# Inverted row sums 16 wide, their spreading on ScalarE, and turned probabilities copied by one engine

## The chip, the cores and the metric

The kernel runs on one core of a Trainium2 chip. The metric is the device time of one execution in microseconds (us), as the median of several runs. Engines are named as in the profile: PE is TensorE's matmuls, PEld its weight loads, DVE is VectorE, ACT is ScalarE, POOL is GpSimd, SP is the engine whose queue starts the DMAs.

## The reference, cut to what matters

Four cross-attention layers act in a chain on x of 4 batches x 1024 tokens x 256, each with 77 keys made from a context of its own batch. The first has 8 heads of 32 and is followed by a state-space scan over the tokens; the second has 16 heads of 64 and a causal mask; the third and the fourth have 16 heads of 16, with a mask each, and the fourth ends in an MLP with a GELU. What the change is about is the softmax and what follows it:

```
# layer 3 of the chain (L2 in the code), 16 heads of 16
m = max(scores, -1)
e = exp(scores - m) * mask
probs = e / (sum(e, -1) + 1e-09)
attn = einsum('bhqk,bhkd->bhqd', probs, vh)      # then @ Wo.T + bo, + residual, layer norm
# layer 4 of the chain (L3 in the code), 16 heads of 16
attn = softmax(where(xa_mask, neg, attn), -1)
out = einsum('bhnm,bmhd->bnhd', attn, v)         # then @ proj_w + proj_b, + x, MLP
```

The kernel leaves the division until after the product with the values: it multiplies each head's 16 output columns by 1 / sum.

## The kernel before, in words

Tokens are worked on in tiles of 128. There are 32 tiles, spread over four lanes; a lane has two PSUM banks of its own (2 * lane and 2 * lane + 1) and its own slice of every SBUF buffer. The first phase (until about 250 us of the span) takes each tile through layer L0 and prepares the scan; the scan runs over all tokens; the second phase takes each tile through L1, L2, L3 and the MLP. Tables of keys and values for L1 to L3 are made for one pair of batches ahead of the second phase, and for the other pair in its middle.

The steps of a lane are a list (`attention_steps`, `lane_steps`), and so are the table building ("a", "b"), the set-up ("i") and the scan ("s"). `MADE_BY` gives each step to one engine. `TURNS` has one string for each engine, written out: character by character it says whose next step the engine issues. So every engine has one fixed order, and the steps wait for each other through semaphores, `done[step]`, that are compared with a step's number in its engine's order.

The steps around the change, for L2 and L3 (`a.name` is "2" or "3"), each for two groups of 8 heads (".0" and ".1"):

- `scores` (PE, L860) fills both banks with 8 x 77 scores; `bound` (DVE, L1378 and L1381) masks them into SBUF; `rowmax` (DVE, L1388), `below` (POOL, L1663), `expo` (ACT, L1196) give the exponentials; `maskmul` (POOL, L1649) is for L2 alone; `rowsum` (DVE, L1399) writes the 8 sums of the group into `mx`.
- `pturn` (PE, L875) turns the 616 probability columns in five tiles of 128, the last with 104 rows. Four go to the lane's first bank, the fifth to the second.
- `pturn_main` (ACT, L1202) copies the first bank, 512 columns, back to SBUF over the probabilities; `pturn_rest` (DVE, L1432) copies the fifth tile, 104 x 128. There are 224 of each, for all four layers.
- `den_eps` (DVE, L1407, L2 alone), then `recip` (DVE, L1420): 1 / sum for 16 heads, written 256 wide into `z`, each head's value 16 times.
- `rturn` (PE, L884) turns these 256 columns, `rec_t` (ACT, L1206) copies them back into `z`.
- `mix` (PE, L918 for L2 and L3, L911 for L1, L907 for L0) is the product with the values; `heads` (DVE, L1443) multiplies it by the turned reciprocals; `proj` (PE, L932) and `resid` (DVE, L1453) follow.

Others that are named below: `turn` (PE, L799) turns normed tokens, from `norm` (DVE, L1366), whose `rstd` is made on POOL (L1624). `fc1` is L968, `fc2` L979, `gelu` L1222. Exp and Gelu need different tables on ScalarE, so each change of function in the scalar order brings a table load.

L0 and L1 invert their sums 8 wide (same line, L1420). `rec` is a buffer of 16 values a lane that L0 and L1 use.

Of the kernel before, what the change touches and what calls it, by code (L numbers as in the profile page):

```python
# [13 lines left out]
P = 128  # L14
H = 256
KC = H // P
KEYS = 77
HG = 8
# [64 lines left out]
def attention_steps(a):  # L83
    if a is L0:
        steps = [("query", "0"), ("query_bias", "0")]
        steps += [(s, "0.0") for s in ("scores", "rowmax", "shift", "expo", "pturn", "pturn_main", "pturn_rest", "mix", "recip", "heads")]
        return steps + [("turn", "0o"), ("turned", "0o"), ("proj", "0"), ("resid", "0")]
# [4 lines left out]
    turns = ["pturn", "pturn_main", "pturn_rest"]  # L92
# [6 lines left out]
    return steps + [("den_eps", a.name)] * (a is L2) + [(s, a.name) for s in ("recip", "rturn", "rec_t", "mix", "heads", "proj", "resid")]  # L99
# [82 lines left out]
def setup_steps():  # L182
    steps = [("ctx_stats", 0), ("ctx_rstd", 0), ("ctx_norm", 0), ("head_masks", 0), ("row_masks", 0), ("value_zero", 0)]
    for n, it in enumerate(ITEMS):
# [7 lines left out]
    "scalar": ("item_act", "turned", "query_bias", "expo", "pturn_main", "rec_t", "u_sb", "gelu", "w2_sb", "wqt_sb", "k1_sb", "vt_sb", "silu", "more_act"),  # L192
    "vector": ("ctx_stats", "ctx_norm", "item_dve", "stats", "aggr", "norm", "bound", "rowmax", "shift", "rowsum", "den_eps", "recip", "weigh",
               "pturn_rest", "heads", "resid", "resume", "wk_sb", "vwo_sb", "k_sb", "v_sb", "carry", "ends", "gap", "agree"),
# [4 lines left out]
def lane_steps(lane):  # L199
# [12 lines left out]
    for n, run in enumerate(second):  # L212
# [19 lines left out]
        "iiiiiiii1ii0iiii0i1ii2ii1ii0iiii2ii2i0i1021032030123001203013211032210123023103310323002103212302133110221012032"  # L232
        "0133132302100321320132031120231012332013012031210123023201013213201320312301032310200312030132112032201321023301"
        "32013012012302130321123012301203231031032102012302013123103122012032013313231212332301312aa23a03aaaaasaasasasasa"
        "saasaasaasaasaasaasaasaasaaasasasaasaaasaasaasaasasaasaasasaasaasasaasaasasaasaa0a231001103132020101020101203110"
        "10200021s3210210101032020001031021013201000220120311312021321210113013023320131022023132032212203120132003102331"
        "3123103333023012012113012030202013102100312003023212102013131320213211021013130321323120202031320322132012201030"
        "2301332131020310332033123102131013002023021012130002310232201231011313021321120112310320330213122021302303223012"
        "22031001023121331302031033201333210230112001320230210101320103213221211313bb312321121132bbbbbb3bb32bb3bb3bb2bb22"
        "bbbbbbbbbbbbbb23bb3bbbbbbbbbb3b3bbb2bb21022012021031202030102013030103101001301333302301020210321101300202131021"  # L240
        "0030021302301223120113132021321101110320321033231220203132032312201220310023021331320130103323313210211031230200"
        "2013102100123000312322103203113120213211021130130233102312202130232301223201230132013030213123103030210331232101"
        "3021300202131021010230200213230210131313202132110211301303123230120202313203223122021031002301233131020310323331"
        "023121310210320020131021003200312312212113133123221231323323221213323232323333233333"),
    "vector": (
        "iii01102201ii2i3iiiii0013ii123021002ii00111021220000331211222132001333320300110330232130000021313112232211122123"
        "2331300233300013132200100010111233202322111132323322100233330031102001200010112013322112223212213331230033031310"
        "0312201010001023132021322112331001233222033330000311220001020111313122211213122332320032333000013103221000011312"
        "032212121113220033122203333330011322101102332020131113322223333sssssssssssssssassasaasasaaasaassaasaassaaasaaass"
        "aaasaaasasasssaasaa000aa0112313122303021100001011001001021112101223222310000222320101010001023300013030021011113"  # L250
        "3331001001210100001131022200003211222221110100002112222100221231111030002303000021313023132132322013333223113323"
        "0222210111001113112033100202203203130330030032023330130221222113222210321111033100301201010101331101200020332233"
        "3112333321123212000020112212231200122231113100020303200002013332311213132322033233123313220022111013103111103102"
        "0030232202303133000300020233311322112220212220102313311100033101110021303110000133223332213133322131012022002032"
        "1121122021022111312033003002203000211130331223322103333223112333222210000131110330111010001323223230210003302002"
        "0311333322112220012222303311203311001000210111133101002012332233311233323103212221112113222121112212333322133223"
        "2333bbb2b3bb232223b33bbb3bbb33bbb2bbbbbbbbbb2b23b32bbbbbb3100011301230220211200000100003102213110133111120000301"
        "0030003233012200201001010322220203010133132111001000111133011100200233223331133332032002110012223121212212012202"
        "1111330003002300001102312332110333223233232311233322200211111300331111000123322003022013303000223000333321122211"
        "2222203113133210011023101110010031103100020232233313221333311030102222003112222121002212111313000200332000033011"  # L260
        "3312221332013232332312133222321011101001113313200213020203032313303000022333030102111222210221220133032311103200"
        "0111100133011100022033221313323213222323310001012103112222012202111313002000330020031103333121322120323332231332"
        "1302222010101311013131120221320330200031030030230020313331222221122202113302031133010121001110103110312000203322"
        "333133322312322211111231122212011122123333223223333322232233332333222233333333333333213"),
    "scalar": (
        "iiiiiiii01iiii1ii02ii2010212033012030031021102213201312333020312300310210112220311233320313200031201102123213012"
        "3320132300102131012023121032332031003201302102121320132132301302300123011012232013133202130023010312011222013123"
        "332133231012a23aa03asaaasaaassassaaaasaassaaasaaaasasaasaasasaasasssssssssssssssss010310210010122021010032010112"
        "3013102300000211022010211201331022103110330232232100231321022100133023013313203312201121001302002311023200313212"
        "2101133022130110303322231220013320121201030033323112003123312102001130022013312003232112201113321032011323002233"  # L270
        "1220031230220113001033231130032123320112001031202013231003122312121133212311bb332bbbbbb2233bb2bb2bbbb33222013002"
        "1330013010130001201023331012020101320100213102300322311210211332021011330032232301220133210212013003302313120032"
        "1332112011320002031102320013231122013312210031103303223212201032312012003133031023132010213312210001320021103322"
        "0023123211011332210301130302322310202133201220301130302331120031233211200110302201102330032232111211332213313232"
        "232213322333332333"),
    "gpsimd": (
        "ii102ii31i020000112232131a3033002a121132223103300011221203321330001022121123333000012121233320130001112223323310"
        "00011221223333101122330a0013212100000111100000001111122202321310022202213333212133332300210002330003103121110300"
        "11110012222211302222231b1333321023330322300003123100020303111100311110132222120102222123033312321103333320003032"
        "2200003311011013301111012222012122212332133322333323301122230000003310001011010031111022123202011222321320333211"  # L280
        "2333033200023023100003113011120031111102222123001222213333320211233033232010030322000130111010330111103222202111"
        "02222211333323102033332000233023210000013111133002111100222121312221221333332233333233323"),
    "sync": (
        "0aaa120aaaaa3aa2aa31aaaaaaaa0011aa2332010312aaaaa23a01a20133220121003302211a30a3aaa0213213aa32113030aa2120aaa0a0"
        "32101b132122213002b0331001bb31b1220333b2023120130032310121022133"),
# [1437 lines left out]
```

## Time and profile before

| | |
|---|---|
| median of 3 runs | 1362.54 us (1361.63 to 1363.4) |
| profiled execution | 1361.59 us |
| its span | 1359.8 us |
| PE, PEld busy | 1272.6, 1036.5 us |
| DVE busy | 1058.6 us, 2140 instructions |
| ACT busy | 683.2 us, 1509 instructions |
| POOL busy | 564.3 us |

How to read it: the span is the time between the first and the last instruction that the profiler recorded, and the execution's time is a little longer. Busy time of an engine is the union of its instructions. A matmul's record goes on until its result is through the array, so records overlap, and a row's mean is more than the step from one matmul to the next. A line of the views groups instructions by the source line of the kernel, and "idle before" is time for which the engine stood still ahead of them, with what let it go on.

### The profile page before, as it was taken

How to read it: one execution, taken by the hardware profiler on the slowest of the kernel's cores; microseconds unless marked ns; L12 is line 12 of the kernel's file. 1: busy time of each engine (PE TensorE's matmuls, PEld its weight loads, DVE VectorE, ACT ScalarE, POOL GpSimd, SP SyncE). 2: the span in 40 equal slices, each digit the busy share in tenths (PEclk: the TensorE clock that was granted, in tenths of full speed). 3: DMA queues.
4: the chain of work that ended last, by engine and by line, in shares of the span. 5: the costliest groups of instructions: out<-in, count | busy, mean ns of one | idle time of the engine just before them, and what ended most of it. 6: DMA issues, size and time to landing. Idle time of an engine off the chain costs nothing.

```text
span 1359.8 us, 25054 instructions
## 1 busy us (share of the span) xinstructions
PE 1272.6 (94%) x9539; PEld 1036.5 (76%) x9539; DVE 1058.6 (78%) x2140; ACT 683.2 (50%) x1509; POOL 564.3 (41%) x696
## 2 busy tenths in 40 slices
PE   7899999998899999999999999999999999999987
PEld 6789988766677777777777777777777777777766
DVE  4677873678788888888888767788888888888883
ACT  4567776223554544555544433554444555555543
POOL 4644432014444454435444311544444444454541
PEclk9999999998999999999999999999999999999999
DMA  4521223010000000000010100000000000000000
GB/s 126 115 86 59 75 83 112 1 14 2 20 24 1 9 1 9 25 1 1 1 36 8 44 2 20 16 11 1 5 24 10 1 1 17 13 5 1 1 10 16
DMA packets 48472, 34.23 MB, mean 25 GB/s; under 512 B 22177, under 2 KB 45536, under 8 KB 48352
## 3 DMA queue, kind: packets, MB, share of 16 engines
q1 hardware_dynamic: 48304, 32.59, 8.6%
q8 instruction: 78, 1.28, 0.4%
q14 instruction: 42, 0.34, 0.1%
q10 hardware_dynamic: 48, 0.01, 0.0%
HBM read 23.26 MB, written 8.39 MB: 23 GB/s over the span
## 4 chain that ended last, share of the span: by engine, by line
PE 67%; DVE 20%; issue 3%; ACT 3%; POOL 3%; DMA 2%; SPq 1%; ACTq 0%; DVEq 0%; POOLq 0%
PE ps L875 7%; PE ps L968 7%; PE ps L979 7%; PE ps L911 7%; DVE zt L1420 6%; PE ps L860 6%; PE ps L932 5%; PE ps L850 5%; PE ps L816 5%; PE ps L918 4%; PE ps L799 3%; DVE mx L1388 2%; PE ps L1075 2%; PE ps L907 2%; DVE mx L1399 2%
## 5 line engine op out<-in xcount | busy, mean ns | idle before, releaser
L1624 POOL TENSOR_TENSOR rstd<-mv,halfneg 128x1 f32<-128x1 f32 x192 | 105.5, 551 | 432.7 <-DVE mv L1357 432.4
L850 PE MATMUL ps<-wk,tt 128*128 128x308 f32 x512 | 145.3, 425 | 1.8 <-ACT tt L1175 0.9
L968 PEld LDWEIGHTS ps<-tt,fc 128*128 128x128 f32 x1024 | 117.8, 192 | 12.4 <-ACT tt L1172 9.9
L968 PE MATMUL ps<-tt,fc 128*128 128x128 f32 x1024 | 124.6, 278 | 0.9 <-ACT tt L1172 0.9
L1196 ACT ACTIVATE pr<-pr 128x616 f32<-128x616 f32 x128 | 91.3, 715 | 62.8 <-POOL pr L1663 37.0
L1663 POOL TENSOR_TENSOR front<-mx,front 128x616 f32<-128x616 f32 x64 | 79.1, 1237 | 98.4 <-DVE mx L1388 98.2
L850 PEld LDWEIGHTS ps<-wk,tt 128*128 128x128 f32 x512 | 93.4, 190 | 33.4 <-issue 3.3
L1172 ACT ACTIVATE tt<-ps,cols 128x128 f32<-128x128 f32 x192 | 76.8, 453 | 81.5 <-PE ps L799 80.5
L1420 DVE RECIPROCAL zt<-mx 128x256 f32<-128x256 f32 x64 | 111.6, 1743 | 0.6
L1637 POOL TENSOR_TENSOR xt<-xt,row_bo 128x256 f32<-128x256 f32 x96 | 70.7, 740 | 85.6 <-PE ps L799 50.1
L1453 DVE TENSOR_TENSOR xt<-xt,ps 128x256 f32<-128x256 f32 x160 | 65.2, 409 | 51.4 <-PE ps L932 25.0
L1663 POOL TENSOR_TENSOR pr<-mx,pr 128x616 f32<-128x616 f32 x64 | 80.3, 1254 | 59.5 <-DVE mx L1388 59.2
L1196 ACT ACTIVATE front<-front 128x616 f32<-128x616 f32 x96 | 68.2, 714 | 68.3 <-POOL front L1663 58.3
L1366 DVE TENSOR_SCALAR zt<-xt,mv,rstd 128x256 f32<-128x256 f32 (+1 forms) x160 | 74.0, 465 | 35.7 <-POOL rstd L1624 35.1
L1202 ACT ACTIVATE pr<-ps 128x512 f32<-128x512 f32 x128 | 75.9, 599 | 48.7 <-PE ps L875 29.9
L860 PE MATMUL ps<-kb,big 64*128 64x308 f32 x512 | 95.9, 465 | 4.2 <-DVE pr L1378 1.6
L1353 DVE BATCH_NORM_STATS2 stat<-xt 128x6 f32<-128x256 f32 x192 | 80.4, 420 | 19.7 <-POOL xt L1658 9.3
L875 PE MATMUL ps<-ident,pr 128*128 128x128 f32 (+1 forms) x640 | 91.3, 275 | 4.3 <-ACT pr L1196 1.8
L1202 ACT ACTIVATE front<-ps 128x512 f32<-128x512 f32 x96 | 56.7, 593 | 58.9 <-PE ps L875 45.1
L875 PEld LDWEIGHTS ps<-ident,pr 128*128 128x128 f32 (+1 forms) x640 | 71.8, 139 | 16.7 <-issue 5.9
L1388 DVE TENSOR_REDUCE mx<-ps 128x8 f32<-128x616 f32 x96 | 75.5, 787 | 10.6 <-PE ps L860 3.9
L1399 DVE TENSOR_REDUCE mx<-front 128x8 f32<-128x616 f32 x96 | 75.0, 782 | 6.3 <-POOL front L1649 4.6
(221 smaller groups left out, 3025.4 us busy)
## 6 DMA issues: line engine op xcount, KB each, us to landing
out_dram<-xt SPq DMA_DIRECT2D x64, 128.0 KB, 1.8
xt<-in_x_dram SPq DMA_DIRECT2D x32, 128.0 KB, 2.3
xt<-out_dram SPq DMA_DIRECT2D x32, 128.0 KB, 2.2
fc<-in_L_xattn_fc_w_dram SPq DMA_DIRECT2D x2, 1024.0 KB, 8.0
wk<-in_L_xattn_wkv_dram SPq DMA_DIRECT2D x4, 512.0 KB, 6.8
front<-in_L_xattn_wkv_dram SPq DMA_DIRECT2D x4, 512.0 KB, 4.3
wo<-in_L_xattn_wo_dram SPq DMA_DIRECT2D x1, 1024.0 KB, 5.7
kb<-in_L_xattn_wq_dram SPq DMA_DIRECT2D x1, 1024.0 KB, 5.5
```

The lines of the kernel that those rows point to most:

```text
L850: last = mm(bank(lane, k)[:, SFROM[k]:SFROM[k] + HB * KEYS], t[:, lane, kc, :], wk[:, kc, b, h0:h0 + HB * KEYS], start=kc == 0, stop=kc == ...
L860: last = mm(bank(lane, k)[:, SFROM[k] + n * w:SFROM[k] + (n + 1) * w], q[half, lane, c * P:(c + 1) * P], kblk[a.name][half, b, c, :, :], s ...
L875: last = turn_in(bank(lane, j // 4)[0:TROWS[j], j % 4 * P:(j % 4 + 1) * P], probs(key, lane)[:, j * P:j * P + TROWS[j]], ident[:, :])
L911: last = mm(o[:, 0:H], pt[j], vwo[0:TROWS[j], b, g, j, :], start=g == j == 0, stop=g == a.groups - 1 and j == TILES - 1)
L968: last = mm(bank(lane, c // 4)[:, c % 4 * P:(c % 4 + 1) * P], fc1[:, kc, c * P:(c + 1) * P], t[:, lane, kc, :], start=kc == 0, stop=kc == ...
L1196: ac(v, v, ACT.Exp, scale=-ATTN[key[0]].scale).then_inc(done["expo"], 1)
L1202: ac(probs(key, run.lane)[:, 0:4 * P], bank(run.lane, 0), ACT.Copy).then_inc(done["pturn_main"], 1)
L1388: v.tensor_reduce(mx[:, run.lane, group(key), :], src, AX.X, ALU.max).then_inc(done["rowmax"], 1)
L1399: v.tensor_reduce(mx[:, run.lane, group(key), :], heads_view(key, run.lane), AX.X, ALU.add).then_inc(done["rowsum"], 1)
L1420: v.reciprocal(dst, src).then_inc(done["recip"], 1)
L1624: p.tensor_tensor(rstd[:, n:n + 1], mv[:, n, 1:2], halfneg[:, :], ALU.pow).then_inc(done["rstd"], 1)
L1663: p.tensor_tensor(p8, each_head(mx, key, run.lane), p8, ALU.subtract).then_inc(done["below"], 1)
```

## The change

The reciprocals of L2 and L3 are taken 16 wide, into `rec`. A new step `widen` on ScalarE spreads them to 256 columns in `z`, and `rturn` waits for it. `pturn_main` copies 640 columns that span both banks, for all four layers, and `pturn_rest` is gone, with every wait for it. (Rows 104 to 127 of the fifth tile are copied too; nothing reads them.) The strings of `TURNS` are new for all engines: the tensor order keeps its 1428 steps, the scalar order has 1090 instead of 1026, the vector order 1879 instead of 2103, gpsimd and sync keep 649 and 176.

```
@@ def attention_steps(a):
-        steps += [(s, "0.0") for s in ("scores", "rowmax", "shift", "expo", "pturn", "pturn_main", "pturn_rest", "mix", "recip", "heads")]
+        steps += [(s, "0.0") for s in ("scores", "rowmax", "shift", "expo", "pturn", "pturn_main", "mix", "recip", "heads")]
...
-    turns = ["pturn", "pturn_main", "pturn_rest"]
+    turns = ["pturn", "pturn_main"]
...
-    return steps + [("den_eps", a.name)] * (a is L2) + [(s, a.name) for s in ("recip", "rturn", "rec_t", "mix", "heads", "proj", "resid")]
+    return steps + [("den_eps", a.name)] * (a is L2) + [(s, a.name) for s in ("recip", "widen", "rturn", "rec_t", "mix", "heads", "proj", "resid")]
@@ TURNS = {
-        "iiiiiiii1ii0iiii0i1ii2ii1ii0iiii2ii2i0i1021032030123001203013211032210123023103310323002103212302133110221012032"
+        "iiiiiiii201ii2iii0ii2ii1ii0ii1ii2ii0ii0i102i03131023200130210211321013032013203031032130210302312301123101322330"
...
@@ def pturn(key, run):
                 if group(key):
                     pe.wait_ge(done["pturn_main"], at("pturn_main", f"{a.name}.0", run))
-                    pe.wait_ge(done["pturn_rest"], at("pturn_rest", f"{a.name}.0", run))
@@ def rturn(key, run):
-                pe.wait_ge(done["recip"], at("recip", key, run))
-                pe.wait_ge(done["pturn_rest"], at("pturn_rest", key + ".1", run))
+                pe.wait_ge(done["widen"], at("widen", key, run))
+                pe.wait_ge(done["pturn_main"], at("pturn_main", key + ".1", run))
@@ def mix(key, run):
                     pe.wait_ge(done["pturn_main"], at("pturn_main", k, run))
-                    pe.wait_ge(done["pturn_rest"], at("pturn_rest", k, run))
@@ def pturn_main(key, run):
-                ac(probs(key, run.lane)[:, 0:4 * P], bank(run.lane, 0), ACT.Copy).then_inc(done["pturn_main"], 1)
+                both = banks(run.lane).rearrange("p k n -> p (k n)")
+                ac(probs(key, run.lane), both[:, 0:TILES * P], ACT.Copy).then_inc(done["pturn_main"], 1)
+
+            def widen(key, run):
+                act.wait_ge(done["recip"], at("recip", key, run))
+                src = rec[:, run.lane, :, :].rearrange("p g h -> p (g h)").unsqueeze(2).to_broadcast([P, 2 * HG, L2.hd])
+                ac(z[:, run.lane, 0:H].rearrange("p (h d) -> p h d", d=L2.hd), src, ACT.Copy).then_inc(done["widen"], 1)
@@ def recip(key, run):
-                    dst = z[:, lane, 0:H].rearrange("p (h d) -> p h d", d=L2.hd)
-                    src = mx[:, lane, :, :].rearrange("p g h -> p (g h)").unsqueeze(2).to_broadcast([P, 2 * HG, L2.hd])
+                    dst, src = rec[:, lane, :, :], mx[:, lane, :, :]
                 v.reciprocal(dst, src).then_inc(done["recip"], 1)
...
-            def pturn_rest(key, run):
-                lane = run.lane
-                dve.wait_ge(done["pturn"], at("pturn", key, run))
-                if key[0] in "23":
-                    dve.wait_ge(done["rowsum"], at("rowsum", key, run))
-                v.tensor_copy(probs(key, lane)[0:TROWS[-1], 4 * P:5 * P], bank(lane, 1)[0:TROWS[-1], 0:P]).then_inc(done["pturn_rest"], 1)
```

## Rows read from the trace of the kernel before

**Rows 1.** The page: the span, and busy time, share and instructions of each engine

```profile
span 1359.8 us, 25054 instructions
...
PE 1272.6 (94%) x9539; PEld 1036.5 (76%) x9539; DVE 1058.6 (78%) x2140; ACT 683.2 (50%) x1509; POOL 564.3 (41%) x696
```

**Rows 2.** Busy time by stretch: stretch, its length, engines' busy us, granted clock, DMA share, GB/s

```profile
0.00:100.00 100.00, 84.13 (x636) 73.93 (x636) 63.44 (x179) 54.46 (x140) 49.96 (x101) 0.98 0.45 111
100.00:200.00 100.00, 99.62 (x822) 91.02 (x821) 79.27 (x212) 72.78 (x185) 45.45 (x72) 1.00 0.23 74
200.00:400.00 200.00, 185.03 (x1163) 146.29 (x1162) 139.93 (x295) 86.61 (x206) 58.91 (x66) 0.97 0.10 28
400.00:1300.00 900.00, 856.37 (x6539) 688.27 (x6539) 743.45 (x1397) 441.71 (x920) 389.37 (x432) 1.00 0.04 10
1300.00:1359.80 59.80, 47.49 (x386) 36.96 (x384) 32.54 (x62) 27.60 (x60) 20.62 (x25) 0.97 0.04 14
```

**Rows 3.** Waits of PE: who waited for whom, us in total, times, the longest

```profile
PE ps L884 <- DVE zt L1420: 36.5, 40, 2.0
PE ps L932 <- DVE tt L1443: 7.3, 13, 1.2
...
PE ps L799 <- DVE zt L1366: 3.2, 6, 1.1
PE ps L875 <- ACT pr L1196: 1.8, 3, 0.7
```

**Rows 4.** Chain of waits around 652 us: start, us, what

```profile
651.83 1.76 DVE zt L1420
653.59 0.04 issue
653.63 0.44 PE ps L884 x2
```

**Rows 5.** The same view around 620 us

```profile
617.58 0.55 PE ps L875 x5
618.12 4.32 PE ps L911 x20
622.45 0.22 PE ps L884 x2
```

**Rows 6.** Waits, of PE's weight loads

```profile
PEld ps L884 <- DVE zt L1420: 52.3, 46, 2.3
```

**Rows 7.** Groups by line, shapes apart: shapes, count, busy us, mean ns, idle before

```profile
L1420 DVE RECIPROCAL zt<-mx 128x256 f32<-128x256 f32 x64 | 111.6, 1743 | 0.6
...
L1196 ACT ACTIVATE pr<-pr 128x616 f32<-128x616 f32 x128 | 91.3, 715 | 62.8 <-POOL pr L1663 37.0 <-DVE pr L1394 25.4
...
L1202 ACT ACTIVATE pr<-ps 128x512 f32<-128x512 f32 x128 | 75.9, 599 | 48.7 <-PE ps L875 29.9 <-DVE mx L1399 18.3
L1388 DVE TENSOR_REDUCE mx<-ps 128x8 f32<-128x616 f32 x96 | 75.5, 787 | 10.6 <-PE ps L860 3.9 <-PE ps L853 3.4 <-PE ps L850 2.9
L1399 DVE TENSOR_REDUCE mx<-front 128x8 f32<-128x616 f32 x96 | 75.0, 782 | 6.3 <-POOL front L1649 4.6 <-ACT front L1196 1.3
L1399 DVE TENSOR_REDUCE mx<-pr 128x8 f32<-128x616 f32 x96 | 74.9, 781 | 4.3 <-POOL pr L1649 2.7 <-ACT pr L1196 1.5
...
L1196 ACT ACT_TABLE_LOAD x34 | 43.6, 1283 | 0.6
...
L1432 DVE COPY pr<-ps 104x128 f32<-104x128 f32 x128 | 35.7, 280 | 19.4 <-PE ps L875 16.9
L1432 DVE COPY front<-ps 104x128 f32<-104x128 f32 x96 | 27.0, 282 | 15.8 <-PE ps L875 14.3
...
L1206 ACT ACTIVATE zt<-ps 128x256 f32<-128x256 f32 x64 | 24.5, 383 | 77.8 <-PE ps L884 77.7
...
L1420 DVE RECIPROCAL rec<-mx 128x8 f32<-128x8 f32 x64 | 12.8, 201 | 1.7
```

More of the change, by code:

```diff
@@ L191 @@
                "w2_mm", "wqt_mm", "k_mm", "wk_mm", "vt_mm", "vwo_mm", "v_mm", "scan_mm", "gap_turn", "more_pe"),
-    "scalar": ("item_act", "turned", "query_bias", "expo", "pturn_main", "rec_t", "u_sb", "gelu", "w2_sb", "wqt_sb", "k1_sb", "vt_sb", "silu", "more_act"),
+    "scalar": ("item_act", "turned", "query_bias", "expo", "pturn_main", "widen", "rec_t", "u_sb", "gelu", "w2_sb", "wqt_sb", "k1_sb", "vt_sb", "silu", "more_act"),
     "vector": ("ctx_stats", "ctx_norm", "item_dve", "stats", "aggr", "norm", "bound", "rowmax", "shift", "rowsum", "den_eps", "recip", "weigh",
-               "pturn_rest", "heads", "resid", "resume", "wk_sb", "vwo_sb", "k_sb", "v_sb", "carry", "ends", "gap", "agree"),
+               "heads", "resid", "resume", "wk_sb", "vwo_sb", "k_sb", "v_sb", "carry", "ends", "gap", "agree"),
     "gpsimd": ("ctx_rstd", "head_masks", "row_masks", "value_zero", "zeros", "rstd", "prebias", "keep", "below", "maskmul", "gain", "offset", "masks", "fold", "vtw_zero"),
@@ L236 @@
[L236 to L244, printed above, removed]
-    "vector": (
[L246 to L264, printed above, removed]
@@ L265 @@
-    "scalar": (
[L266 to L275, printed above, removed]
@@ new lines @@
+        "2123010320023102301212311022101203231033120312131200231023013223103123302310312012031020310203213103220133123020"
+        "1302121300213021021132310210232033102103231002120310211321031230321233132312013203233101203aa23aaaasaaasaasaasaa"
+        "saasaaasaasaaasaaasaasaaasasasasasaasaasasaasaasasaasaasasaasaasasaasaassasaasaa02a30101103213020101201021010132"
+        "10202100012321120100s3030032001012101200000121020131312021321101102303132302131220203132032212220130130023021331"
+        "3201301330331201311201230230020213102100032003213122132030113120213211111032032033123010220231320321222201301002"
@@ new lines @@
+        "0313200202131021001320020122310230131313202132111301102303232131202020313203221302221301002301213313020310332332"
+        "012131103102320020131021030312321322323131101202132131323321212232332323233332323333"),
+    "vector": (
+        "i0011ii2220133iiii220ii0ii11ii300002ii00020110221133222111211002333313100300332003200111011332212211003312223323"
+        "3330201130002200003311221121233021121012223300113332323000010110012211332212122221333030333331100002233110100102"
+        "2220111313313220022333233000011022000331112102221231112122300323331331003220000001011122332121121221002333233113"
+        "0333221103322110003130212233323ssssssssssssasasasassasasaasasaaassaassaasaasaaasaaasaasasasasssasaa000a0a1111203"
+        "0332213210000001010111212311022222221230000111100333230013101000103200102321320110000120302211120000011110010002"
+        "1122220022123111130033000020032211333120212213333312331322202011111300312110033003222321030000223000333311122120"
+        "2021311132220100303311201131103100220033231213332330000222111113022222022102111133003302203000021112133320123233"
+        "3311332302202211111100331122200330202331030000220030133331221122202221033301110303021110113011310200203322133331"
+        "2223310101000213212221220201113213033000002030323321222201133333113323022202110001011311002311213032223013003023"
+        "00233313011122222100221100312033331021111031131022002002331323112233231013211222232122111133332231322323bbbbbb33"
+        "2bbb3bbb2b3b33bb323bbbb22bbbbb22bb3bbb3bbbb100103031312222003311200000000121121111103220000332301030020200001200"
+        "1011232010331101030213011101113013200020332233313313112122100020032122221220201131313322000310000022121131233233"
+        "0333123313222002111111013103222030323200130300002320033303212111002221101123223310303200111133101210200203231333"
+        "2212032331201100222211032202013311110000233022230002111113322303333312130322320200111110111300223323022130330000"
+        "2300203333121211222020022033101013303112111133011100022033223313211132022103030102222123222010111133000303202003"
+        "0111231322310233332311233322202011110011333110232233030022010000220030133313221221220202300131131203310101113311"
+        "012000203332332333121112223112122232332213211113333222322333322333222223333333013333323"),
@@ new lines @@
+    "scalar": (
+        "iiiiiii2i02ii1ii0ii120ii0120133201300021301110231220310323321030032010311123212230132302303010210210112322103123"
+        "2313012303002310112302233131022310320010320103212133230121230132000123101102223102133203120300132011130221231323"
+        "32130323101230a2a3saaaaasaasaaaasasaaassaaaasaaasaaasaasaasasassssssssssssssssssss011023001012120012103020110002"
+        "1321110033022000002112230020111011132210301100233332230122203321102210013030032333121030133121211102003020021310"
+        "3200223322111231101320213113003203323212020231321022100130030323311300321233121201100123000231102320013232211211"
+        "310302123031103033223202202133200122010010313323331132010123130112200132002031102320201221312311133221b3113bbb2b"
+        "bbb233323bbbb222bbbb33232201303332010301001102001001032330101212110012032000131032200312311222110133022131103032"
+        "0223331220203132012201010303230333121003211331201112003200201310223002122233110113310221311302300232332010223203"
+        "1012021130300233331120031232301120011130020321103220021221312301113302210311330032322312220013320122100313000321"
+        "3313003221332201101110302020131032030322122132311113221331331322222233233333322333"),
@@ new lines @@
+    "gpsimd": (
+        "ii201ii0i3300002211111222303330010a11223323213000a01122112233330001102212133332000101123122333020012011122332330"
+        "00102112233323101102332a0011233200001011112000002210022111001110322221133302232103331332200003322000013130111003"
+        "1112b10022221031122232013332231123330322103000323000033111011300321111021222201102222031132333220133333200003222"
+        "1300010311131003011111202222031122223113223332333323320113020000031230000111100301112110022213120222213133023232"
+        "1333332002000133220000331011110303111102222021110220232213332131233033200002332131000031110010332111102122221010"
+        "20232231323321321333322001003303200003113120100131111120223221132223233132202333323331332"),
@@ L1293, in more_act @@
                     act.sem_inc(more_r, MORE)
-            steps = {"item_act": item_act, "turned": turned, "query_bias": query_bias, "expo": expo, "pturn_main": pturn_main, "rec_t": rec_t, "u_sb": u_sb,
+            steps = {"item_act": item_act, "turned": turned, "query_bias": query_bias, "expo": expo, "pturn_main": pturn_main, "widen": widen, "rec_t": rec_t, "u_sb": u_sb,
                      "gelu": gelu, "w2_sb": w2_sb, "wqt_sb": wqt_sb, "k1_sb": k1_sb, "vt_sb": vt_sb, "silu": silu, "more_act": more_act}
@@ L1540, in _ @@
                      "shift": shift, "rowsum": rowsum, "den_eps": den_eps, "recip": recip, "weigh": weigh,
-                     "pturn_rest": pturn_rest, "heads": heads, "resid": resid, "resume": resume, "wk_sb": wk_sb, "vwo_sb": vwo_sb, "k_sb": k_sb,
+                     "heads": heads, "resid": resid, "resume": resume, "wk_sb": wk_sb, "vwo_sb": vwo_sb, "k_sb": k_sb,
                      "v_sb": v_sb, "carry": carry, "ends": do_ends, "gap": do_gap, "agree": do_agree}
```

18 lines of the change are left out of this document (7 added, 11 removed).

## The prediction

> **What bounds the kernel now.** I read the page first. TensorE (PE) is busy for 94% of the span, VectorE (DVE) for 78%, ScalarE (ACT) for 50%, GpSimd for 41% [rows 1]. One engine is nearly full, so what matters is when it stands idle and who lets it go on. The table by stretch says where: from 400 to 1300 us, where the four lanes turn round in their second phase, PE is busy for 856.37 of 900 us, so 43.6 us are idle; from 200 to 400 it is 15.0 us, and in the last 59.8 us 12.3 us [rows 2]. The 16 us before 100 us are loads and set-up that the change doesn't touch, and from 100 to 200 us PE is at 99.6%. PE's clock was granted at 0.97 to 1.00 throughout, its full level. So 70.9 us of PE idleness (15.0 + 43.6 + 12.3) can be won at all.
>
> The waits of PE come next. One row is half of that: the turn of the inverted row sums (L884) waited 36.5 us, in 40 of its 64 places, for the 256-wide reciprocal of L1420. The next rows behind VectorE are 7.3 us (L932, for the product of L1443) and 3.2 us (L799, for the norm of L1366); those behind a ScalarE copy or exponential are small, 1.8 us the largest [rows 3]. The chain of waits around 652 us shows such a place: the reciprocal takes 1.76 us, a step of 0.03 to 0.04 us, and L884 starts. It also shows a second cost. The two turns of L884 then take 0.44 us [rows 4]; where they ran in PE's stream without a wait they took 0.22 us [rows 5]. A stall thus costs 0.22 us more than its idle time, which PE's busy time hides: 40 x 0.22 = 8.8 us. PE's weight loads bear this out from the other side: they stood idle 52.3 us for the same reciprocal, 15.8 us more than the matmuls [rows 6].
>
> **The change, part by part.**
> The reciprocal. It goes from 256 columns (1743 ns, 64 times, 111.6 us) to 16. The 8-wide one takes 201 ns [rows 7]; between the two lies (1743 - 201) / 248 = 6.2 ns a column, so 16 columns take 201 + 50 = 251 ns. Bounds: 201 ns, and 402 ns for two 8-wide ones in a row. VectorE gets back 64 x 1.49 = 95.5 us.
>
> The spreading (widen) is new on ScalarE: 256 columns, SBUF to SBUF, the source read with each value repeated. The 256-wide copy out of PSUM takes 383 ns, 616 columns in SBUF take 715 ns, and 256 to 512 columns of copies differ by (599 - 383) / 256 = 0.84 ns a column, so from the SBUF row 715 - 360 x 0.84 = 413 ns [rows 7]. I take 410. Bounds: 383 and 715. It costs ScalarE 64 x 0.41 = 26 us.
>
> The copies of the turned probabilities. VectorE's fifth-tile copies go: 35.7 + 27.0 = 62.7 us for 224. ScalarE's go from 512 to 640 columns: 599 + 128 x 0.84 = 707 ns, bounded by 599 (the columns free) and 735 (the 616-wide SBUF row plus 24 columns); 224 x 0.108 = 24 us. The copy now crosses from one bank into the next; no row shows such a read by ScalarE, though VectorE's 616-wide reductions do it at 787 ns against 781 to 782 ns out of SBUF, so I add nothing [rows 7]. PE gives up one wait for each, and the next turn into those banks waits for one engine, 0.11 us later than the ScalarE part was ready, but no longer for a copy that stands in VectorE's queue.
>
> Totals: VectorE 1058.6 - 95.5 - 62.7 = 900 us (66% of the old span), ScalarE 683.2 + 26 + 24 = 733 us (54%). The new scalar order has 31 changes from Exp to Gelu where the old has 34; the six table loads saved (three each way, 1283 ns each [rows 7]) give 7.7 us back: 725 us. Neither becomes a bound; GpSimd's and the queues' DMAs have the same steps, 649 and 176, in a new order.
>
> The latency. From the sums to the turn it was 1.74 us; it becomes 0.25 + 0.04 + 0.41 = 0.70 us, 1.04 us shorter. The old wait has a mean of 0.91 us (36.5 / 40) and a longest of 2.0, so most of the 40 waits end. In the new scalar order widen stands directly behind the lane's own 640-wide copy in 55 of 64 places, and that copy waits for the second turn: turn, 0.71, 0.41, L884, or 1.12 us. In the new tensor order one step or more stands between that turn and L884 in 63 of 64 places (two or more in 47), each of 0.22 us (two turns) to 4.32 us (L911) of PE work [rows 5], so this too is mostly covered. I leave 4 us of waits there.
>
> The sum. Waits at L884: -36.5 + 4 = **-32.5**. Refills of those stalls, nearly all: **-8**. Other waits behind VectorE (7.3 + 3.2 = 10.5): with VectorE some 15% emptier I halve them, **-5**. ScalarE is 7% fuller and its copies later by 0.11 us; its waits on PE in rows 3 could grow: **+2**. Together -43.5 us on the profiled execution's 1361.6 us (span 1359.8 and 1.8 around it) gives 1318; the median of the three runs is 0.9 us above that execution, so 1319. What is no term of the sum: the new order itself. It is written out by hand or by a planner, and I read only counts from it; it can keep or lose some us everywhere.
>
> **Rivals.**
> 1. Half only. PE's four lanes are a closed loop: a stall taken away at L884 comes back at the next late input of the same lane (L932, L799, L875), because the lanes' order is fixed and a lane that gets ahead waits at its next step. For it: VectorE still has 900 us of work, and the steps after L884 (rec_t, heads, proj) keep their latency. Against: those rows are short today although VectorE is full. Price: half of 32.5 + 8 + 5 is 22.8, less the 2 us lost: 1362.5 - 21 = 1342. Chance 0.15, for 1332 to 1348.
> 2. More than the sum. All idle time from 200 us on is 70.9 us; if the order makes use of the free VectorE as the stretch from 100 to 200 us does (99.6% busy at 79% VectorE and 73% ScalarE), only some 5 us stay, and 12 us of refills go: 1362.5 - 66 - 12 = 1285. That stretch is filled with table building which waits for nobody, so it proves little. PE's own busy time hides room too: the 0.22 us of each refill in rows 4. The Trainium skill (Trainium Kernel Development and Optimization, Best Practices) goes further: matmul busy time is a poor measure of distance to the limit, and the busy share of weight loads is a good one. By that rule the 76% of PEld in rows 1, 688.27 of 900 us in the steady stretch [rows 2], would mean far more room than PE's 5%; a gain of 78 us would be no surprise to it. Chance 0.12, for 1280 to 1298.
> 3. Slower: ScalarE is in the way. Widen is queued in order. If it, or the 640-wide copy, stood behind a table load with its exponential (1.28 + 0.72 = 2.0 us) at all 64 places, L884 would come 2.0 - 1.04 = 1.0 us later than now: 64 us lost, 1427. It decides from an added ScalarE delay of 1.04 us a place (where the shorter reciprocal is eaten), with nothing else won. Against: only 4 of the 64 stand right behind an exponential in the new order, and ScalarE is half idle. Chance 0.04.
> 4. No effect, within 0.2%: the stalls of L884 only stand in for a bound elsewhere, such as the latency from norm to norm. Against: PE at 95% leaves no room for such a loop. 1362.5. Chance 0.03.
>
> The forecast itself (1298 to 1332) has 0.66. The range reaches from 1296, where all 10.5 us of the other waits behind VectorE, all of L884's and the lesser stalls are gone, to 1347, which takes in nearly all of rival 1. The unknown costs are small inside this: widen at 715 instead of 410 ns adds 0.3 us to a chain that is covered, at most 64 x 0.3 = 20 us. Outside stay most of rival 2 (0.10), rivals 3 and 4 (0.07) and the end of rival 1 (0.02). About 0.2% is what a measurement of this kernel can tell from no change: faster 0.93, same 0.03, slower 0.04.
>
> **What would show it.** L1420 at 250 ns; widen near 410; the copies near 707; VectorE at 900 us and ScalarE at 725. PE's waits at L884 down to a few us, their releaser now the spreading on ScalarE; idle time of PE from 400 to 1300 us down from 43.6 to about 15; PE's busy sum itself down by 8 or more. I am wrong if L884 waits 15 us or more for ScalarE, if the waits at L932 and L799 grow, if the new copy takes more than 800 ns, or if PE's idle time is gone but its busy time has grown by as much.

## The result, and the profile after

The changed kernel takes 1291.15 us (median of 4 runs, 1290.36 to 1291.56); the kernel before took 1362.97 us beside it. The ratio is 0.9474, with a 95% interval of 0.9457 to 0.949: 71.8 us less, where 43.5 were forecast, and 4.9 us below the low end of the range.

The page of the changed kernel, its span and engines, to be held against [rows 1]:

```profile
span 1289.6 us, 24640 instructions
...
PE 1253.4 (97%) x9539; PEld 1033.4 (80%) x9539; DVE 929.1 (72%) x1916; ACT 719.4 (56%) x1567; POOL 565.1 (44%) x696
```

PE's idle time went from 1359.8 - 1272.6 = 87.2 us to 1289.6 - 1253.4 = 36.2 us, 51.0 less, and its busy time fell by 19.2 us for the same 9539 matmuls. The two make the 70.2 us of the span.

Busy time by stretch, in the columns of [rows 2] (the steady stretch ends earlier now):

```profile
0.00:100.00 100.00, 89.77 (x691) 79.28 (x692) 65.67 (x174) 60.88 (x154) 52.71 (x106) 1.00 0.41 99
100.00:200.00 100.00, 99.38 (x816) 89.69 (x815) 77.07 (x198) 71.95 (x177) 42.45 (x68) 1.00 0.26 80
200.00:400.00 200.00, 190.06 (x1275) 151.38 (x1274) 134.50 (x286) 94.15 (x223) 66.81 (x76) 1.00 0.11 30
400.00:1200.00 800.00, 793.01 (x6092) 648.06 (x6092) 598.58 (x1159) 445.88 (x913) 367.89 (x406) 1.00 0.04 12
1200.00:1289.60 89.60, 81.20 (x673) 65.04 (x671) 53.27 (x103) 46.56 (x102) 35.23 (x41) 0.98 0.03 10
```

In the steady stretch PE stands still for 7 of 800 us, where it was 43.6 of 900. There is also a gain before 100 us, 89.77 busy for 84.13, in a stretch that the prediction called untouched.

Waits of PE in the changed kernel, to be held against [rows 3] (L881 is the turn of the reciprocals, L797 the turns of tokens, L928 `proj`):

```profile
PE ps L734 <- DMA vwo<-in_L_xattn_W_qkv_dram: 6.5, 2, 6.1
PE ps L797 <- DVE zt L1368: 4.2, 9, 0.9
PE ps L881 <- ACT zt L1204: 2.3, 4, 1.1
PE ps L928 <- DVE tt L1437: 1.8, 4, 0.6
```

The turn of the reciprocals waits 2.3 us in 4 places instead of 36.5 in 40. Another row behind VectorE fell as well: the turns of tokens waiting for the residual sum `resid` (L1453 before, L1447 now). In the kernel before it is the third row behind VectorE, between the 7.3 and the 3.2 us that the prediction names; in [rows 3] it is under the dots:

```profile
PE ps L799 <- DVE xt L1453: 6.0, 4, 3.3
```

```profile
PE ps L797 <- DVE xt L1447: 1.0, 3, 0.4
```

Of the 6.0 us, 4.9 lie before 100 us; of the 1.0 us, 0.7.

The groups that the change made, shapes apart, against [rows 7]:

```profile
L1199 ACT ACTIVATE pr<-ps 128x640 f32<-128x640 f32 x128 | 88.9, 704 | 32.5 <-PE ps L872 25.4 <-DVE mx L1401 6.9
...
L1192 ACT ACT_TABLE_LOAD x31 | 39.8, 1283 | 0.6
...
L1204 ACT ACTIVATE zt<-rec 128x256 f32<-128x256 f32 x64 | 26.4, 412 | 16.0 <-DVE rec L1421 15.9
...
L1421 DVE RECIPROCAL rec<-mx 128x16 f32<-128x16 f32 x64 | 15.4, 243 | 1.0
```

So the price of each instruction was right: 243 ns for 251, 412 for 410, 704 for 707. What was not right is what they are worth. Three parts came at once (the short reciprocal with its spreading; the single copy; the order), so the experiments take them apart.

### The profile page after: what moved, and what is told of

Same layout as the page of the kernel before. It is cut to its first block, busy times and chain, and to the rows that moved or that the text cites. A ratio compares the mean times of both kernels' runs of the same rounds, so it can differ in the third digit from the quotient of the medians.

```text
span 1289.6 us, 24640 instructions
## 1 busy us (share of the span) xinstructions
PE 1253.4 (97%) x9539; PEld 1033.4 (80%) x9539; DVE 929.1 (72%) x1916; ACT 719.4 (56%) x1567; POOL 565.1 (44%) x696
## 4 chain that ended last, share of the span: by engine, by line
PE 75%; DVE 8%; issue 6%; ACT 3%; POOL 3%; SPq 2%; DMA 2%; ACTq 0%; DVEq 0%; POOLq 0%
PE ps L907 10%; PE ps L872 8%; PE ps L848 8%; PE ps L975 8%; PE ps L964 8%; PE ps L858 6%; PE ps L928 6%; PE ps L814 5%; PE ps L914 5%; PE ps L797 3%; PE ps L903 2%; SPq L620 1%; DVE mx L1390 1%; DVE zt L1368 1%; PE ps L1071 1%
## 5 line engine op out<-in xcount | busy, mean ns | idle before, releaser
L964 PEld LDWEIGHTS ps<-tt,fc 128*128 128x128 f32 x1024 | 117.8, 192 | 11.3 <-ACT tt L1168 10.5
L1447 DVE TENSOR_TENSOR xt<-xt,ps 128x256 f32<-128x256 f32 x160 | 65.7, 412 | 78.0 <-PE ps L928 39.3
L1368 DVE TENSOR_SCALAR zt<-xt,mv,rstd 128x256 f32<-128x256 f32 (+1 forms) x160 | 80.8, 507 | 48.8 <-POOL rstd L1618 48.3
L1199 ACT ACTIVATE pr<-ps 128x640 f32<-128x640 f32 x128 | 88.9, 704 | 32.5 <-PE ps L872 25.4
L1199 ACT ACTIVATE front<-ps 128x640 f32<-128x640 f32 x96 | 67.2, 702 | 58.2 <-PE ps L872 46.3
L1401 DVE TENSOR_REDUCE mx<-pr 128x8 f32<-128x616 f32 x96 | 75.0, 783 | 16.0 <-POOL pr L1643 11.0
```

The source lines that it names most:

```text
L964: last = mm(bank(lane, c // 4)[:, c % 4 * P:(c % 4 + 1) * P], fc1[:, kc, c * P:(c + 1) * P], t[:, lane, kc, :], start=kc == 0, stop=kc == ...
L1199: ac(probs(key, run.lane), both[:, 0:TILES * P], ACT.Copy).then_inc(done["pturn_main"], 1)
L1368: v.tensor_scalar((z0 if key == "0" else z)[:, lane, own], x[:, slot(run), own], mv[:, n, 0:1], rstd[:, n:n + 1], ALU.subtract, ALU.mult). ...
L1401: v.tensor_reduce(mx[:, run.lane, group(key), :], heads_view(key, run.lane), AX.X, ALU.add).then_inc(done["rowsum"], 1)
```

## The experiments

In all of them "the kernel before" was timed beside the variant, and it gave 1363.45, 1364.42 and 1365.19 us in the three sets. A variant of one set compared with one of another is good to about 2 us: taken by ratios, the differences below move by 0.5 to 1.5 us. Where a step had to be put into an order that does not know it, its place was read from the trace of the kernel before or of the changed kernel; the expectations say how.

### The two parts of the change under the old order

`b_recip`, the reciprocal and the spreading alone:

```
         for at, key, lane, no in WIDENS:
+            self.order["scalar"].insert(at, ("widen", key, runs_of(lane)[no]))
...
-                    dst = z[:, lane, 0:H].rearrange("p (h d) -> p h d", d=L2.hd)
-                    src = mx[:, lane, :, :].rearrange("p g h -> p (g h)").unsqueeze(2).to_broadcast([P, 2 * HG, L2.hd])
+                    dst, src = rec[:, lane, :, :], mx[:, lane, :, :]
```

> The kernel before, with its old order of steps, and one part of the change: reciprocal 16 wide, spread by ScalarE; each spreading stands in the scalar order where ScalarE was when the reciprocal began in the trace. The fifth-tile copies stay on VectorE. Theory 1 (the removed waits carry the gain, whatever the order): the waits of the reciprocals' turn fall from 36.5 us to under 10, and the time to about 1320. Theory 2 (a fixed order made for the old lengths gives a removed stall back at the next late input; the new order is what collects it): no more than half, 1340 or above.

Measured: 1311.68 us, ratio 0.9624 (0.9606 to 0.9643), 51.8 us less. Theory 1 holds for this part, and more came than the 43.5 us that were forecast for everything. Waits of PE (L901 is the turn of the reciprocals, L949 `proj`, L816 the turns of tokens):

```profile
PE ps L901 <- ACT zt L1224: 5.7, 11, 1.3
...
PE ps L949 <- DVE tt L1464: 1.9, 7, 0.5
PE ps L816 <- DVE zt L1388: 1.9, 3, 1.1
```

The row of 36.5 us is down to 5.7, and L949, which was 7.3, is down to 1.9: the waits of others fell too.

`b_copy`, the single copy alone (the three moved copies and the changed waits are not shown):

```
         self.order = {e: in_turn(e) for e in MADE_BY}
+        self.order["vector"] = [x for x in self.order["vector"] if x[0] != "pturn_rest"]
...
-                ac(probs(key, run.lane)[:, 0:4 * P], bank(run.lane, 0), ACT.Copy).then_inc(done["pturn_main"], 1)
+                both = banks(run.lane).rearrange("p k n -> p (k n)")
+                ac(probs(key, run.lane), both[:, 0:TILES * P], ACT.Copy).then_inc(done["pturn_main"], 1)
```

> The kernel before and its old order, with the other part alone: one ScalarE copy of 640 columns over both banks, no VectorE copy (three of the 640-wide copies are moved one or two steps forward in the scalar order, since the turn of the reciprocals now waits for them). VectorE gets 62.7 us back, ScalarE takes on 24. Theory 1: 5 to 15 us gained, 1350 or so, since the long reciprocals' waits stay but begin earlier. Theory 2: within 5 us of 1362.

Measured: 1343.17 us, ratio 0.9853 (0.9837 to 0.987), 20.3 us less, above both expectations. A line of its page, and its longest wait of PE:

```profile
PE 1267.7 (95%) x9539; PEld 1034.2 (77%) x9539; DVE 1018.9 (76%) x1916; ACT 706.9 (53%) x1509; POOL 564.7 (42%) x696
```

```profile
PE ps L886 <- DVE zt L1422: 27.5, 34, 2.1
```

VectorE got only 1058.6 - 1018.9 = 39.7 us back, not the 62.7 of the copies' rows: a row adds up its instructions, and the records overlap. In the kernel before, the copy that starts at 658.33 us takes 0.26 us, and the next instruction starts at 658.50, 0.09 us before it ends. With the copies' records struck out, the union of VectorE's records in that trace is 1019.4 us, close to the 1018.9 of `b_copy`. The wait for the long reciprocals stays, but 9 us shorter: VectorE comes to the reciprocal sooner.

`b_both`, the two together, still under the old order:

> All operations of the change under the old order of steps. Theory 1: the two parts together bring 50 us or more, 1312 or below, and the new order only the last 20. Theory 2: 1335 or above, and the new order more than half of the 71.7 us.

Measured: 1312.19 us, ratio 0.9632 (0.9615 to 0.9649). The first part was worth 51.8 us, the second 20.3, both 51.3. Once the reciprocal is short, the single copy brings nothing under this order. Neither theory had that; theory 1's number is met, theory 2's is far off. A row of PE's waits shows part of the reason (L903 is the turn of the reciprocals, L1221 the single copy):

```profile
PE ps L903 <- ACT front L1221: 4.7, 4, 2.3
```

Under the old order the turn now waits 4.7 us for the longer copy. `b_recip` has no such row, and neither has the changed kernel.

### The order alone, and each part taken back under the new order

`a_both_back` is the changed kernel with its order and all old operations (256-wide reciprocal, no spreading, 512-wide copy, `pturn_rest` inserted into the vector order). `a_recip_back` takes back only the first part, `a_copy_back` only the second:

```
         self.order = {e: in_turn(e) for e in MADE_BY}
+        self.order["scalar"] = [x for x in self.order["scalar"] if x[0] != "widen"]
...
-                    dst, src = rec[:, lane, :, :], mx[:, lane, :, :]
+                    dst = z[:, lane, 0:H].rearrange("p (h d) -> p h d", d=L2.hd)
+                    src = mx[:, lane, :, :].rearrange("p g h -> p (g h)").unsqueeze(2).to_broadcast([P, 2 * HG, L2.hd])
```

```
         self.order = {e: in_turn(e) for e in MADE_BY}
+        for at, key, lane, no in RESTS:
+            self.order["vector"].insert(at, ("pturn_rest", key, runs_of(lane)[no]))
...
-                both = banks(run.lane).rearrange("p k n -> p (k n)")
-                ac(probs(key, run.lane), both[:, 0:TILES * P], ACT.Copy).then_inc(done["pturn_main"], 1)
+                ac(probs(key, run.lane)[:, 0:4 * P], bank(run.lane, 0), ACT.Copy).then_inc(done["pturn_main"], 1)
```

> The new order of steps with all old operations: reciprocal 256 wide, no spreading, fifth-tile copies back on VectorE, each where VectorE was when ScalarE's copy began in the trace. It shows the order alone. Theory 1: the order alone is worth 10 to 20 us, 1345 to 1352. Theory 2: an order is worth something only with the lengths it was made for, 1355 to 1375.

> The changed kernel with its new order, the reciprocal 256 wide again and no spreading; the single 640-wide copy stays. The six runs so far: both parts under the old order -51 us, the first alone -52, the second alone -20, the order alone -4, all three -71. If the parts overlap because both relieve the same VectorE queue ahead of the turn of the reciprocals, taking the reciprocal back costs most: 1335 to 1345. If the new order is what makes the single copy pay, it is nearer 1325.

> The changed kernel with its new order, short reciprocal and spreading, the fifth-tile copies back on VectorE. If the single copy is worth nothing once the reciprocal is short (as under the old order, 1312.2 against 1311.7), this stays within 5 us of 1291. If it pays under the order that was made for it, 1300 to 1312.

Measured: 1359.56 us (ratio 0.9965, 0.9954 to 0.9977), 1338.43 us (0.9812, 0.9795 to 0.983) and 1298.43 us (0.9519, 0.9501 to 0.9537). The first lies in theory 2's range. The second lies where it should if taking the reciprocal back costs most. The third misses both of its expectations, a little above "within 5 us of 1291" and below "1300 to 1312". With the runs above, all eight cases are there:

| | old order | new order |
|---|---|---|
| old operations | 1363 | 1359.6 |
| single copy | 1343.2 | 1338.4 |
| short reciprocal, spread | 1311.7 | 1298.4 |
| both | 1312.2 | 1291.2 |

The new order is worth 4 to 5 us where the reciprocal is long, 13.3 where it is short, and 21.0 with both. That it gives little with the long reciprocal isn't a matter of badly inserted steps: `a_recip_back` has none inserted, and there it gives 4.7. So theory 2 is right of the order (made for the new lengths, it gives little without them) and wrong of the operations (they hold 51 of 72 us without it).

The order's gain has two places. The scan is the one serial stage that each variant passes once, so its start is a milestone. These rows give the scan's step on ScalarE: minimum, median and maximum ns, first and last start in us. In this order they are of the kernel before, of `b_both`, of the changed kernel and of `a_both_back`:

```profile
L1280 ACT ACTIVATE zt<-ps x32: 277/277/279, 216.4 to 269.1; 128x128 f32<-128x128 f32 x32
```

```profile
L1304 ACT ACTIVATE zt<-ps x32: 277/278/279, 216.8 to 269.5; 128x128 f32<-128x128 f32 x32
```

```profile
L1282 ACT ACTIVATE zt<-ps x32: 277/278/317, 209.5 to 263.7; 128x128 f32<-128x128 f32 x32
```

```profile
L1328 ACT ACTIVATE zt<-ps x32: 277/277/320, 210.2 to 264.3; 128x128 f32<-128x128 f32 x32
```

The new operations don't move the scan (216.4 and 216.8); the new order does (209.5), with the old operations as well (210.2). Some 7 us of the order's 21 are thus won in the first phase by order alone. Most of it is the wait for `resid` before 100 us that stands above: 4.9 us in the kernel before and 5.0 in `b_both`, 0.7 in the changed kernel and 0.3 in `a_both_back`. The other 14 are in the second phase, and there the order needs the new lengths: with the old ones it is ahead by 6.2 us at the scan, and at the end by 3.9 in the medians and by nothing in the two profiled executions (both spans are 1359.8 us). The waits of PE in `a_both_back` (L927 is the turn of the reciprocals, L842 the turns of tokens, L975 `proj`; L1468 is the reciprocal, L1480 the fifth-tile copy) tell where those went:

```profile
PE ps L927 <- DVE zt L1468: 11.5, 14, 2.6
PE ps L842 <- DVE zt L1414: 10.0, 19, 1.6
PE ps L975 <- DVE tt L1491: 9.9, 12, 1.7
PE ps L927 <- DVE front L1480: 8.4, 10, 2.1
```

The long reciprocal still costs, but the loss is now spread over several rows, all behind a VectorE that is as busy as before (1060.6 us for 1058.6).

### Latency or occupancy

The short reciprocal does two things: the turn's input comes a microsecond sooner, and VectorE is free 1.5 us sooner for whatever stands behind. Both kernels start from `b_recip` (1311.7 us). `b_recip_long` gives VectorE its work back but not the turn its delay; `b_recip_late` does the reverse:

```
                 v.reciprocal(dst, src).then_inc(done["recip"], 1)
+                if key in ("2", "3"):
+                    for n in (11, 1):
+                        dve.wait_ge(spare_no, spares[0])
+                        spares[0] += 1
+                        v.reciprocal(spare[:, 0:n * 16].rearrange("p (h d) -> p h d", d=L2.hd),
+                                     mx[:, lane, :, :].rearrange("p g h -> p (g h)")[:, 0:n].unsqueeze(2).to_broadcast([P, n, L2.hd])).then_inc(spare_no, 1)
```

```
                 act.wait_ge(done["recip"], at("recip", key, run))
...
+                for _ in range(3):
+                    act.wait_ge(spare_no, spares[0])
+                    spares[0] += 1
+                    ac(spare[:, :].rearrange("p (h d) -> p h d", d=L2.hd), src[:, 0:11, :], ACT.Copy).then_inc(spare_no, 1)
                 ac(z[:, run.lane, 0:H].rearrange("p (h d) -> p h d", d=L2.hd), src, ACT.Copy).then_inc(done["widen"], 1)
```

> The kernel before with the short reciprocal and the spreading (1311.7 us), and right behind each short reciprocal two further ones on VectorE, 11 and 1 heads wide, into a spare buffer that nobody reads: VectorE is occupied for about 1.75 us at each place as before, but the turn need not wait for it. Theory latency (the 36.5 us of waits were the price): no more than 10 us lost, 1312 to 1322. Theory occupancy (what counts is what stands behind the reciprocal in VectorE's queue): most of the 52 us lost again, 1340 to 1360.

> The same kernel (1311.7 us) with three further spreadings of 11 heads into a spare buffer ahead of the real one on ScalarE, each waiting for the one before: the turn comes some 1.2 us later, about when it came before the change, while VectorE stays free; ScalarE has some 75 us more. Theory latency: most of the 52 us lost again, 1345 to 1365. Theory occupancy: no more than 15 us lost, 1312 to 1327.

The edits do nearly what they are for. `b_recip_long` has VectorE busy for 1049.2 us, 77.6 more than `b_recip` (971.6), where the kernel before has 87.0 more. In `b_recip_late` the spread values are ready 1.76 us after the reciprocal began, on average, as against 0.75 us in `b_recip` and 1.74 in the kernel before.

Measured: `b_recip_long` 1343.66 us (ratio 0.985, 0.9832 to 0.9867), 32.0 us worse than `b_recip`. `b_recip_late` 1356.86 us (0.9951, 0.9932 to 0.997), 45.2 us worse. Neither theory stands alone. The late kernel has ScalarE busy for some 60 us more as well (764.8 us for 704.5), so a control has the same three spare copies behind the real one (the `ac(z...)` line moved ahead of the loop):

> Control for the run with the late spreading (1356.9 us): the same three spare spreadings a place on ScalarE, but behind the real one, so that the turn need not wait for them. If ScalarE's 60 us more of work were what cost 45 us there, this is about 1350 too. If it was the later turn, this stays within 10 us of the kernel without spare spreadings (1311.7): 1312 to 1322.

Measured: 1328.22 us (0.9736, 0.9719 to 0.9752), 16.5 us worse than `b_recip`, above its expectation: ScalarE, at 58% busy, isn't free. If the added work cost the same in both, the turn's lateness itself would be 1356.9 - 1328.2 = 28.6 us. It is likely to cost less in `b_recip_late`, because the control makes something late of its own. Behind the real spreading its copies stand in the way of the lane's next ScalarE step, `rec_t`, which begins 0.67 us after the turn's end on average (0.32 in `b_recip`, 0.35 in `b_recip_late`), and PE waits 7.0 us at `mix` (L937) for `pturn_main` (L1221), where `b_recip_late` has 3.7. So I read 28.6 us as a lower bound of the lateness, and 45.2 us as an upper one.

The waits of PE, first the turn of the reciprocals in `b_recip_late`, then `b_recip_long`'s (L951 `proj`, L818 turns of tokens, L903 the turn of the reciprocals):

```profile
PE ps L903 <- ACT zt L1232: 37.7, 39, 2.3
```

```profile
PE ps L951 <- DVE tt L1474: 14.7, 21, 1.2
PE ps L818 <- DVE zt L1390: 8.6, 13, 2.1
...
PE ps L903 <- ACT zt L1226: 5.9, 11, 1.3
```

The first row is nearly the row of the kernel before (36.5, 40, 2.0), with another releaser: lateness brings the old stall back. In `b_recip_long` that row stays at 5.9, and the price appears elsewhere: 14.7 us at `proj` (1.9 without the extra work) and 8.6 at the turns (1.9). Lateness of 28.6 us or more and occupancy of 32.0 us sum to at least 60.6, more than the 51.8 that both together are worth: the two overlap. As I read it, in the kernel before the stall at the turn covered the others: VectorE caught up while PE stood there, so the later steps found their inputs ready. No run shows this by itself.

## Why the prediction was right and wrong

**The bound and the main cause** were right: PE's waits on the long reciprocal were the largest loss, and they are gone (2.3 us left, 4 forecast). The scalar order has 31 table loads each way, as counted. ScalarE's busy time was forecast at 725 and is 719.4. VectorE's was forecast at 900 and is 929.1: the sum took the records of the copies and the reciprocals off in full, though they overlap with their neighbours' (the first part gave back 87.0 us instead of 95.5, the copies 39.7 instead of 62.7).

**The order, "no term of the sum", is the step that failed.** The sum put it at nothing, and the only reason given was that just counts had been read from it. In the kernel as changed it is worth 21.0 us: some 7 before the scan, independent of the operations, and 14 after it. This is what took the result out of the range: the operations alone, under the old order, come to 1312.2 us, well inside it. Of the 28.3 us that the sum fell short by, 7.8 are the operations' (51.3 for 43.5) and 20.5 come with the order. The worth is not the order's alone, for with the old operations it is 4 us; what was missing is a term for the two together. Two readings of the rows went before this. The 16 us of PE's idle time before 100 us were called loads and set-up that the change doesn't touch, but 4.9 us of them were waits for `resid`; that idle time fell by 5.6 us (84.13 to 89.77 busy). And the row of these waits, 6.0 us in all, was passed over when "the next rows behind VectorE" were named.

**"Other waits behind VectorE, halved: -5"** was mis-sized, and is the second step that failed. It sized VectorE's occupancy by the 10.5 us that PE visibly waited for two of its other products (16.5 us with the third row). By `b_recip_long` it is 32.0 us. A wait that is hidden behind a longer one has no row, so the rows of the kernel before did not give this number; the busy shares (78% beside PE's 94%, with a fixed order between them) were a hint. The sum suffered less than that, since lateness and occupancy overlap: the first part was worth 51.8 us, against 45.5 for the terms of the sum that it stood for (32.5, 8, 5), of which some belonged to the copies.

**The term for the stalls**, -32.5 and -8 for refills, 40.5 together, fits what was measured, a lateness between 28.6 and 45.2 us.

**"ScalarE fuller: +2"** was too small as well. 57 us of work added to ScalarE (761.2 for 704.5) cost 16.5 us (`b_recip_busy`). The single copy adds 24 us to it and frees 39.7 us of VectorE, not 62.7; under the old order with the short reciprocal gain and price cancel (1311.7 and 1312.2 us), with 4.7 us of waits for the copy at the turn. Under the new order those waits are gone, and the copy is worth 7.3 us (1298.43 to 1291.15). Whether those waits are the whole of the difference was not tried.

**Rival 1** (half only, the stall comes back elsewhere) is refuted for the whole change, but its mechanism was real in reverse: other stalls come up when this one alone is removed and VectorE stays full (`b_recip_long`). In the changed kernel the turns' wait for the norm grew only from 3.2 to 4.2 us, and `proj`'s fell from 7.3 to 1.8. **Rival 2** (more than the sum, 1280 to 1298, chance 0.12) is what happened, and mostly in its way: 7 us of idleness in the steady stretch, and PE's busy time down by 19.2 us, of which 8.8 were forecast as refills. Its terms are not met, though: from 200 us on 25.3 us of idleness stay, not 5, and the 5.6 us before 100 us are none of its terms. I also quoted the Trainium skill there (Trainium Kernel Development and Optimization, Best Practices), that the busy share of weight loads and not of matmuls tells the distance to the limit. The trace agrees in part. The time did fall by more than PE's idle time did, and the share rose from 76% to 80%. But at 648.06 of 800 us in the steady stretch, 81%, PE has only 7 us of idleness left: no change of the waits could fill the missing 19%. Whether the same matmuls could follow each other more closely no run here shows. **Rival 3** (ScalarE in the way) is refuted for the spreading in this order (L881 waits 2.3 us), and `b_recip_late` shows its price where the input is late: 45 us. **Rival 4** (no effect) is refuted by the 71.8 us.

## What to carry to other kernels

When a bound engine stalls mostly in one row, that row is not an upper limit of what the slow producer costs: it can hide shorter waits on the same producer. Estimate latency and occupancy apart, and test them apart: one variant that keeps the producer busy after its result is out, one that delivers late on another engine, and a control for the work which the second adds. Look in the control's trace for what it makes late itself; here it gave a bound and not a number. Where every engine runs a written-out order, a change of lengths and the order made for it are two changes that do not add up; time the eight combinations, or at least the new operations under the old order.

## What the runs showed of the hardware that was not expected

PE's clock. [Rows 2] give 0.97 for two stretches of the kernel before, which the prediction took for full level. Looked at in slices, the loss sits in a few short pieces. Of the kernel before, PE's busy time and granted clock in five stretches:

```profile
60.00:71.50 11.50, 11.50 (x83) 0.85 0.60 194
310.00:320.00 10.00, 7.98 (x39) 0.83 0.01 2
320.00:330.00 10.00, 8.51 (x59) 0.83 0.01 2
340.00:350.00 10.00, 6.54 (x56) 0.85 0.00 1
1340.00:1350.00 10.00, 6.62 (x49) 0.83 0.04 14
```

A mean of 0.83 over 10 us is a third of it at the lower of the two levels, 1.2 GHz, and the rest at 2.4. Four of the five pieces are where PE was busy for only 6.5 to 8.5 of 10 us, and the one from 60 us on follows the stretch from 40 to 60 us with 16.5 of 20. Being less busy doesn't always bring it: from 1320 to 1330 us PE was busy for 8.18 us at 1.00. Of the four stretches of the changed kernel below only one, near its end, has the lower clock:

```profile
320.00:330.00 10.00, 8.01 (x75) 1.00 0.02 4
330.00:340.00 10.00, 8.66 (x77) 1.00 0.00 0
340.00:350.00 10.00, 9.37 (x67) 1.00 0.01 2
1270.00:1280.00 10.00, 8.36 (x62) 0.83 0.16 52
```

Five pieces lose 0.15 x 11.5 + 3 x 0.17 x 10 + 0.15 x 10 = 8.3 us of full-rate time, one loses 1.7. So up to 6.6 us of the 19.2 us by which PE's busy time fell can be the clock. The piece at 60 us is in the profiled executions of both the kernel before and `b_both`, and in none of a kernel with the new order, so 1.7 us of what the order wins ahead of the scan can be this. Some of it reaches the end of the span: the four executions of `b_both` had a mean clock of 0.997, 0.996, 0.995 and 0.992 and took 1311.32, 1311.36, 1313.01 and 1315.58 us, so that 0.005 of the clock (6.6 us of full-rate time) goes with 4.3 us. By that, and by the mean clock of 0.995 for `b_both` and 0.9995 for the changed kernel, an estimate for the clock's share of the order's 21 us is 4. That stalls bring the lower clock on is a reading; it was not tried by itself.

On VectorE, the busy time of a row of short instructions overstates what leaving them out frees: 62.7 us in two rows, 39.7 us in the engine's total.
